# Two added waits: seven weight loads and eleven small loads are asked for once the first pair of transposes has landed

## The reference

```
nx = ln(x) ; q, k, v = nx @ wq, nx @ wk, nx @ wv        # 8 heads of 32
x1 = x + softmax(q k^T / sqrt(32) + bias(adj)) v @ wo
x  = x1 + gelu(ln(x1) @ w1) @ w2
for l in 0, 1:                                          # relation layers
    q, k = x @ Wq[l].T, x @ Wk[l].T                     # 128 wide
    x = ln(x + (masked softmax(q k^T / sqrt(128)) x) @ Wc[l].T)
```

## Time and profile before

| | before |
|---|---|
| median of 3 runs | 2104.08 us (2099.52 to 2104.42) |
| the profiled execution | 2106.19 us, its span 2103.9 us |
| busy share of the span | PE 89%, DVE 81%, ACT 74%, POOL 48% |
| mean granted TensorE clock | 0.969 |

### The profile page before, as it was taken

One profiled execution on the slowest core, in us unless ns is written; L12 is line 12 of the kernel. 1 busy time (PEld: TensorE's weight loads), 2 busy tenths in 40 slices (PEclk: granted clock), 3 DMA queues, 4 the chain that ended last, 5 costly groups with the idle time before them and its releaser, 6 DMA issues.

```text
span 2103.9 us, 44316 instructions
## 1 busy us (share of the span) xinstructions
PE 1877.8 (89%) x15704; PEld 1351.8 (64%) x15704; DVE 1699.8 (81%) x3398; ACT 1563.6 (74%) x2996; POOL 1019.8 (48%) x1304
## 2 busy tenths in 40 slices
PE   4778899999999999999999999999999999999884
PEld 2545567666666666666666676666666666666662
DVE  3766788888888888888888888888888888888653
ACT  1466677778877777888777778877777788777651
POOL 2012335555544555555445555554555555445575
PEclk9698899999999999999999999999999999999997
DMA  6223344433344443333444443344444334444211
GB/s 151 66 46 81 91 101 101 103 85 82 86 110 101 111 101 95 84 84 91 101 111 111 101 86 82 85 101 101 111 103 104 82 82 87 108 101 86 66 36 41
DMA packets 441610, 192.46 MB, mean 91 GB/s; under 512 B 347760, under 2 KB 416368, under 8 KB 441392
## 3 DMA queue, kind: packets, MB, share of 16 engines
q1 hardware_dynamic: 440368, 188.04, 38.1%
q0 software_dynamic: 544, 0.80, 0.3%
q10 hardware_dynamic: 480, 0.79, 0.2%
HBM read 38.55 MB, written 16.78 MB: 26 GB/s over the span
## 4 chain that ended last, share of the span: by engine, by line
PE 61%; ACT 14%; DVE 10%; POOL 9%; issue 4%; DMA 1%; SPq 1%; DVEq 0%; POOLq 0%; ACTq 0%
PE ps L327 17%; PE ps L329 16%; PE ps L328 16%; PE ps L1296 6%; POOL area L543 4%; PE ps L1361 3%; DVE st L746 2%; DVE area L759 2%; ACT L683 2%; ACT cs L704 2%; POOL hid_l L334 2%; DVE area L899 2%; ACT L704 2%; POOL rs L538 2%; POOL ve L536 2%
## 5 line engine op out<-in xcount | busy, mean ns | idle before, releaser
L662 ACT ACTIVATE area<-area,nmax 128x128 f32<-128x128 f32 x1024 | 312.6, 390 | 17.0 <-DVE nmax L874 16.3
L536 POOL TENSOR_TENSOR ve<-mv,eps_cols 128x4 f32<-128x4 f32 x128 | 62.4, 487 | 479.2 <-DVE mv L751 479.0
L334 POOL TENSOR_TENSOR hid_l<-area,hid_h 128x512 f16<-128x512 f32 x128 | 156.5, 1223 | 284.7 <-ACT hid_h L686 284.7
L327 PE MATMUL ps<-w_h,hid_h 128*128 128x256 f16 x1024 | 279.2, 273 | 13.6 <-POOL hid_l L334 12.5
L329 PE MATMUL ps<-w_h,hid_l 128*128 128x256 f16 x1024 | 279.0, 272 | 0.0
L328 PE MATMUL ps<-w_l,hid_h 128*128 128x256 f16 x1024 | 279.0, 272 | 0.0
L683 ACT ACTIVATE area<-ps,b_col 128x512 f32<-128x512 f32 x256 | 176.1, 688 | 44.7 <-PE ps L329 38.0
L327 PE MATMUL ps<-rot_h,w_h 128*128 128x512 f16 x512 | 198.7, 388 | 8.6 <-ACT area L683 5.4
L328 PE MATMUL ps<-rot_l,w_h 128*128 128x512 f16 x512 | 197.5, 386 | 0.0
L329 PE MATMUL ps<-rot_h,w_l 128*128 128x512 f16 x512 | 197.5, 386 | 0.0
L543 POOL TENSOR_TENSOR area<-area,cwb_row 128x256 f32<-128x256 f32 x128 | 89.9, 732 | 198.5 <-ACT area L712 198.5
(11 more groups left out here) (200 smaller groups left out, 5911.3 us busy)
## 6 DMA issues: line engine op xcount, KB each, us to landing
qkS<-qk SPq DMA_DIRECT2D x378, 128.0 KB, 2.3
xin<-in_x SPq DMA_DIRECT2D x32, 512.0 KB, 4.6
adj_in<-in_adj SPq DMA_DIRECT2D x64, 256.0 KB, 2.8
out<-x SPq DMA_DIRECT2D x30, 512.0 KB, 2.8
area<-in_L_gnn_w SPq DMA_DIRECT2D x1, 1024.0 KB, 7.2
area<-in_L_gnn_w SPq DMA_DIRECT2D x2, 512.0 KB, 10.3
rot_h<-sA_h SPq DMA_TRANSPOSE x64, 2.8
rot_l<-sA_l SPq DMA_TRANSPOSE x64, 2.7
```

The source lines that it names most:

```text
L327: pe.matmul(dst, lh, rh, start=start, stop=False, **kw)
L334: eng.tensor_tensor(hid_l[:, c % RING, :], hidden[:, c % 2, :], hid_h[:, c % RING, :], ALU.subtract).then_inc(done, 1)
L662: last = act.activation(sc[:, b % 2, h], sc[:, b % 2, h], ACT.Exp, bias=nmax[:, b, h:h + 1])
```

## The change

Two waits are added. SP waits until both transposes of the first group have landed before it issues the seven loads of `weights_of_layers`. POOL waits for the same before the eleven loads of `more_columns`. Both are for group (0, 0) alone, so each is there once in the program.

```diff
                         turn(g, xT_h, xT_l, sN_h, sN_l, a_xT, d_xT, m_xT)
                         if g == (0, 0):
+
+                            sp.wait_ge(m_xT, TURN)
                             weights_of_layers()
...
                         rsqrt(g, NORMS[stage])
                         if stage == "N" and g == (0, 0):
+
+                            pool.wait_ge(m_xT, TURN)
                             more_columns()
```

## The result

| | before | changed |
|---|---|---|
| median of 6 runs | 2104.03 us (2099.52 to 2104.95) | 2096.11 us (2092.31 to 2097.87) |
| ratio | | 0.9964 (95% interval 0.9952 to 0.9977) |
| the profiled execution | 2106.19 us, span 2103.9 us | 2095.89 us, span 2093.7 us |
| mean granted clock | 0.969 | 0.970 |

The changed kernel is 7.9 us shorter; 6.5 us had been forecast. A second set (5 and 10 runs) gave 2096.52 against 2104.36, ratio 0.9961 (0.9946 to 0.9975): 7.8 us again.

The account below looks back on a forecast made before the run. The start was taken as serial, PE waiting 9.6 us for the first `xT_l` transpose, slowed by loads sharing the DMA engines. A 6.5 us shift, other terms zero, gave 2104.1 - 6.5 = 2097.6 us, range 2093.5 to 2102.

Parts of the forecast that it names:

- The rival that the first pair is slow by itself: First transposes: slow because first, wait stays at 9 us, loads come later, 2104 to 2105; nothing gained had chance 0.06.
- The price, 2.7 us instead of 9.24: First `xT_l` transpose: lands in the median time of its 34 undisturbed fellows, so Q.k0 starts 6.54 us earlier.
- The bad case: First `xT_l` transpose: still takes 4.5 us with its neighbours gone, so the gain is only 4.7 us.
- The bounds of 4.7 and 7.2: Gain at Q.k0's start: 4.7 us if the transpose takes 4.5 us, 7.2 if the weight split alone limits it.
- The shift stays to the end: Whole kernel: a start 6.5 us earlier is an end 6.5 us earlier, unless a held load becomes late.
- The sum: Whole kernel: -6.5 us from the earlier start, with zero for late weights, rows and copies of q and k.
- the bad case: Relation weights and wo: land at 29.6 us, wanted by PE at 29.9, so hidden by 0.3 us.
- the good case: Relation weights and wo: land at 24.5 us, hidden by 5 us before PE's first relation transpose.
- SP's issues shrink without crowded rings: SP's seven held loads: issuing takes 4 to 6.7 us instead of 6.7, none of them over 1 us.
- The 6.5 us put on q0's work: POOL's software queue to 60 us: its loads cost 10.8% of all DMA engines' time, 6.5 us.
- the rival on the other side: PE's clock: longer at the lower level, 13 us more cancels the gain; slower by clock or late load 0.05.
- The same 8 us after the new start: PE's clock: the lower level (1.2 GHz) lasts 8 us from Q.k0's start, as before the change.

Follow-up runs that it names:

- e1: Changed kernel with only SP's wait kept: seven loads held, POOL's eleven asked for as before; 2103.62 us against 2105.59 before, ratio 0.9988.
- e2: Changed kernel with only POOL's wait kept: its eleven loads held, SP's seven follow the transposes at once; 2097.64 us, ratio 0.9961.
- e3: Changed kernel with both waits, but POOL's moved behind its five columns, so only its six rows are held; 2098.36 us, ratio 0.9960.

## Why the prediction was right, step by step

- **The wait at the start ends on the transpose, and the transpose is slow because of what runs beside it.** Right, shown by e1, e2 and the changed kernel's 2.73 us. The rival that the first pair is slow by itself is refuted.
- **The price, 2.7 us instead of 9.24, so 6.54 us.** Right: 6.51 in the first profiles, and 9.66 to 2.74 in the second. PE waited 2.2 us for it, where some 3 had been forecast. The bad case was priced wrongly: halfway between 2.7 and half of 9.2 is 3.65 us and not 4.5. The bounds of 4.7 and 7.2 with half of 4.9 give 2094.4 to 2101.9 and not 2093.5 to 2101. The measured 2096.1 lies in either.
- **The shift stays to the end.** Right: the medians differ by 7.9 us. "Every step stands 6.5 us earlier" was too exact: in the first profiles the lead is 6.8 us at A.S0 and 9.8 at 290 us.
- **What was mis-sized.** The sum lacks 0.45 to 0.56 us of DVE's norm, which POOL's issuing had slowed; the prediction took POOL's issues as free for others. The slowed transpose varies (9.2 and 9.7 in two profiles of before), and the first profile had the smaller of the two. With 9.45 as the mean, the sum is 6.7 + 0.6 = 7.3 us. The remaining 0.6 us lie within the 2.9 us by which the stretch from 60 to 278 us varies.
- **The held loads are hidden.** Right, and by more than the bad case: 3.8 us for the weights, where 0.3 to 5 had been given (the 24.5 of the good case has no working), and 7.9 us for the rows, where 4 had been.
- **SP's issues shrink without crowded rings.** Right: 3.3 us, under the 4 to 6.7 expected, none over 1 us. In e3, where the rows ran beside them, two grew again (1.26 and 1.74 us). That full rings are the reason is argued; no row shows a ring.
- **Both groups of loads counted alike in the argument.** This was loose. The prediction cited both groups for the earlier trace rows, and only POOL's matters: of the seven loads 15 packets had moved at 24.0. Near-equal shares were also a poor sign of turns, since from 17.5 to 20 us q0 had 101.2% and q1 0.3%. The 6.5 us put on q0's work were 8.4% of 60 us = 5.0 in the changed kernel; it changed nothing, since no reader waited.
- **The clock.** Its scatter was named, and the rival on the other side did not come true. "The same 8 us after the new start" held in one profile (8.7 us) and not in the other (4.4).
- **The chances.** 0.44 for faster and 0.51 for within 0.3% rested on 6.5 us lying almost on that bound. The ratio is 0.9964, and the whole interval, 0.23% to 0.48%, contains the bound, so the runs put it just beyond without settling it.

## What to carry to other kernels

A transfer on the critical path that takes three times its usual time is a matter of what else the DMA engines serve, and the shares of the queues tell which queue to hold back. Here loads in the same queue behind it could stay where they were; those in another queue, above all rows spread over partitions, had to wait for its semaphore or be moved behind it into its own queue. When reading an experiment of this kind, count the packets in the stretch of the transfer first: loads that begin only as it ends say nothing about queues. Before holding a load back, take its first reader and its landing time from the trace: here 3.8 us of slack proved real when they were overdrawn.

## What the runs showed of the hardware

- Six spread rows, 0.79 MB, held the 16 engines for 5.0 us beside the transposes. The transpose took 8.64 us beside them and 9.24 and 9.66 with SP's loads behind it as well, against 2.73. It took 5.60 beside plain loads of the same size in the same queue, and 2.73 with the spread rows behind it in its own queue, asked for 1.8 us later.
- A packet of the spread rows took 0.63 us, one of the plain loads 0.451 x 2.5 x 16 / 139 = 0.13 us.
- While POOL issued software transfers, four DVE operations (128x256, f32, two scalars for each partition) took 1.94 us instead of 1.38, in five profiles against nine. In all five the first of them took 0.89 us and ended 0.1 us after POOL's first issue; DVE's `sN_l`, beside the later issues, took 1.23 us in before and 1.22 in the changed kernel. The Trainium skill (SBUF — State Buffer, the "DVE blocks DMA" trap) tells of the other direction, that a DVE operation holds up POOL's descriptor writing. POOL's column issues of 0.70 to 0.72 us were no longer beside DVE's work than in the changed kernel.
- The granted clock reads 1.00 in the rows until the first change of level is recorded (at 47 us before, at 40 us in the changed kernel), although matmuls of 0.63 us, as against 0.38 later, show the lower level. At the start of a trace the durations are the better witness.
